# Row sums of the router weights by one matmul on chip instead of a pass through DRAM, and several steps moved in the order of a Strassen-like pipeline

## The chip, the cores and the metric

The kernel runs on one core of a Trainium2 chip. The metric is device time in microseconds (us), the median of several executions. TensorE is PE in the profile, VectorE is DVE, ScalarE is ACT, GpSimd is POOL, SyncE is SP.

## The reference

The input x is 4 x 1024 tokens of 1024 features. Each token is normalized (mean and variance over its features) to xn, and two branches follow:

```
g    = sigmoid(xn @ gate_w.T + gate_b)
u_g  = xn * g
s_t  = running recurrence over the sequence of b*u_g with decay tanh(a)
y    = c*s + (d + low_rank(mean over sequence of u_g)) * u_g
p    = softmax(xn @ wr.T)            (8 experts), top 2, weights normalized
h    = silu(silu(xn @ w1.T) @ w3.T) @ w2.T
out[index_k of a token] += weight_k * h[token]     (rows 0 to 7 only)
result = x + y * silu(out)
```

The scatter lands in rows 0 to 7 of the first batch alone, since an expert's number is used as a row. So everything but those 8 rows is a copy of x. What is needed in full is h for all 4096 tokens, the router's choice for all tokens, and the mean of u_g over the first batch.

## The kernel before

**The products.** Each 1024 x 1024 x 1024 product is done with seven half-size products (Strassen's scheme in Winograd's form) instead of eight. Every operand is split in a high part and a low part (`h`, `l`), both in fp32r, and each step is three matmuls: high by high, high by low, low by high (`three`, lines 926 to 928). There are nine stages, n = 0 to 8: stages 0 to 3 are x @ w1.T for the four batches, stage 4 is the gate for the first batch, stages 5 to 8 are the product with w3. A stage has seven products (n, i), each of four tiles j, each tile of 12 matmuls of 512 columns. `TILES` lists them by (n, p, j), where p is the position of the product in its stage. Every engine's program is one loop over this list, and `at` = (p, j) says at which tile an engine issues each other step; an engine takes its steps strictly in this order and waits at each for its semaphores. So a place in the list is an order on that engine's own queue, and no time.

**The steps around the products.** DVE forms the sums of blocks that the scheme needs (`x_sum(n, k)`, `w_sum`), ACT rounds them to the high part (`high`, `weights`), DVE subtracts to get the low part (`low(n, i)`, `low_weights`). Each works on a 128 x 2048 tile. DVE also adds finished PSUM tiles to running sums (`evict`). Product (n, i) waits once, ahead of its first matmul, for `low(n, i)` and `low_weights` (`x_in`, `w_in` in `product`). Within DVE's loop at stages 4 and 5 the order was:

```
(0,1): x_sum(n,1)            [stage 4: then two_greatest()]
(0,3): x_sum(n,2), x_sum(n,4)
(1,0): w_sum(n-3,4), low_weights(n-3,2)
(1,1): low(n,2), x_sum(n,3)
(1,2): low_weights(n-3,3)
```

**The router.** `logits(n, b)` multiplies raw x block b (a, c, b, d) by wr, 32 small matmuls each. They run after tile (1,3) in stage 0 and after tile (0,3) in stages 1 to 3. `logits_turned` transposes them to tokens by experts on DVE. The x of the two batches of stages 0 and 1 is raw, so their logits are corrected afterwards: `logits_normalized` subtracts mean times the row sum of wr and multiplies by the inverse deviation, 12 short linked DVE steps; `two_greatest` then picks the experts and `shares` their weights. The row sums of wr came from ACT: job "wr" in `JOBS` loads wr, line 740 sums its rows, SP writes the 8 sums to DRAM (`sums_out`, line 510) and reads them back to all partitions (`sums_back`, line 514). `row_sums` jobs also give the token statistics and the row sums of w1.

**The aggregation.** `aggregate(n, i, of)` multiplies activated tiles by the router's weights into two PSUM banks, 8 small matmuls per j. In stage 8 the ones of i = 1, 4, 5 run after tile (6,1), the one of i = 6 at the very end, before `last_product`.

Of the kernel before, what the change touches and what calls it, by code (L numbers as in the profile page):

```python
# [5 lines left out]
P = 128  # L6
D = 1024
KT = D // P
TOK = 4096
SEQ = 1024  # L10
UT = 1024
HT = 512
E = 8
# [7 lines left out]
GATE = 4  # L21
L2 = 5
# [7 lines left out]
FOLDED = tuple(n for n in SOURCE if SOURCE[n] < RAW)  # L30


JOBS = [(u, r) for u in (2, 3, 0, 1) for r in range(KT)] + [("wr", 0)]
JOBS += [("w1", r) for r in range(KT)]
PLACES = 9
BANKS = 5

# [115 lines left out]
PART = counts(*((b, k) for b in "ac" for k in range(PIECES[b])))  # L153


def program(nc, x, xT, xa, wB, w11, w1, wr, w2T, small, out):
    loads, loaded = {}, [0] * PLACES
    for n in range(NN):
        for b in "acbd" if n else "bd":
# [16 lines left out]

    xh_d = nc.dram_tensor("xh_d", (2, 2, P, 4, HT), F32).ap()
    H_d = nc.dram_tensor("H_d", (NU, 2, 2, P, 4, HT), F32).ap()
    sw_d = nc.dram_tensor("sw_d", (E, 1), F32).ap()
    mv_d = nc.dram_tensor("mv_d", (2 * NU, 2, HT), F32).ap()  # L180

    with ExitStack() as ctx:
        def sb(name, shape, dt=F32):
            return ctx.enter_context(nc.sbuf_tensor(name, shape, dt))
# [4 lines left out]
        def sem(name):  # L189
            return ctx.enter_context(nc.semaphore(name))  # L190
# [27 lines left out]
        nm = sb("nm", [P, 1])  # L218
        acs = sb("acs", [P, 2 * NU, 2, 4])
        ws = sb("ws", [P, KT])  # L220
        wrs = sb("wrs", [P, 1])
        sw = sb("sw", [P, E])
        hb = sb("hb", [P, KT])
        aa = sb("aa", [P, KT])
        us = sb("us", [P, 2, KT])
# [18 lines left out]
        def piece(buf, c0, m, n):  # L244
            return buf[:, c0:c0 + m * n].rearrange("p (m n) -> p m n", n=n)
# [22 lines left out]
        lgp = [ps(f"lgp{i}", [P, HT]) for i in range(2)]  # L268
        spare = ps("spare", [P, HT])
        acc = [lgp[1], spare]  # L270

        s_row = [sem(f"s_row{i}") for i in range(2)]
        s_pl = [sem(f"s_pl{i}") for i in range(PLACES)]
# [17 lines left out]
        s_wh = sem("s_wh")  # L291
        s_wo = sem("s_wo")
        s_s = sem("s_s")
        s_sws = sem("s_sws")
        s_swl = sem("s_swl")
        s_fd = sem("s_fd")
        s_fs = sem("s_fs")
        s_mm = sem("s_mm")
# [40 lines left out]
        def job_buf(q):  # L339
            return rows[:, q % 2, :]  # L340
# [4 lines left out]
        def job_done(on, q):  # L345
            on.wait_ge(s_st2, q + 1)
# [113 lines left out]
        def bank_free(on, n, i, j):  # L460
# [7 lines left out]
            else:  # L468
# [4 lines left out]
            [(0, *at) for at in ((2, 1), (2, 3), (3, 0), (3, 1), (3, 3), (4, 0), (4, 2), (5, 0), (6, 0), (6, 2))]  # L473
            + [(1, *at) for at in ((0, 1), (0, 3), (1, 2), (2, 2), (3, 2), (4, 1), (5, 1), (6, 0), (6, 2))]
            + [(2, *at) for at in ((0, 1), (0, 3), (1, 2), (2, 2), (3, 0), (3, 2), (4, 1), (5, 1), (6, 0), (6, 2))]
            + [(3, *at) for at in ((0, 1), (0, 3), (1, 1), (1, 3), (2, 2), (3, 0), (3, 2), (4, 1), (5, 0), (5, 2), (6, 0),
                                   (6, 2))])}
        turned_at = {(0, 4, 0): 4, (0, 6, 0): 5, (2, 1, 3): 6, (2, 5, 1): 7, (3, 1, 3): 0, (3, 2, 3): 1, (3, 3, 3): 2,
                     (3, 5, 1): 3}
        back_at = {(0, 4, 1): (2, 0), (0, 6, 1): (2, 1), (2, 2, 0): (3, 0), (2, 5, 2): (3, 1)}  # L480
# [11 lines left out]
        def _(eng):  # L492
            on = Waits(eng)

            def row(q):
                if q >= 2:
                    job_done(on, q - 2)
                of, r = JOBS[q]
                if of == "wr":
                    src = wr  # L500
                elif of == "w1":
                    src = w1[r * P:(r + 1) * P, :]
                else:
                    r0 = BATCH[of] * SEQ + r * P
                    src = x[r0:r0 + P, :]
                eng.dma_start(job_buf(q)[0:E, :] if of == "wr" else job_buf(q), src).then_inc(s_row[q % 2], 16)

            def sums_out():
                job_done(on, JOBS.index(("wr", 0)))
                eng.dma_start(sw_d, wrs[0:E, :]).then_inc(s_sws, 16)  # L510

            def sums_back():
                on.wait_ge(s_sws, 16)
                eng.dma_start(sw[:, :], sw_d.rearrange("e o -> (o e)").partition_broadcast(P)).then_inc(s_swl, 16)

            def first_block(b, k):
                src = xa[k] if b == "a" else part(xT[BATCH[0], 1, 0], b, k)
# [76 lines left out]
            for t in range(4, len(TILES)):  # L594
# [58 lines left out]
                    stats_out(turned_at[(n, p, j)])  # L653
                if (n, p, j) in back_at:
                    stats_back(*back_at[(n, p, j)])
                if n == GATE - 1 and at == (2, 0):
                    sums_out()
                if n == GATE - 1 and at == (3, 0):
                    sums_back()
                if (n, p, j) in save_at:  # L660
                    save(save_at[(n, p, j)])
                if n == NN - 1:
# [57 lines left out]
        def _(eng):  # L720
# [11 lines left out]
            def row_sums(q):  # L732
                job_loaded(on, q)
                of, r = JOBS[q]
                buf = job_buf(q)
                if of == "w1":
                    eng.activation(buf, buf, ACT.Copy, accum_out=ws[:, r:r + 1]).then_inc(s_st2, 1)
                    return
                if of == "wr":
                    eng.activation(buf[0:E, :], buf[0:E, :], ACT.Copy, accum_out=wrs[0:E, :]).then_inc(s_st2, 1)  # L740
                    return
                total, square = (acs[:, 2 * of + r // 4, e, r % 4:r % 4 + 1] for e in range(2))
                link(eng.activation(buf, buf, ACT.Copy, accum_out=total))  # L743
                link(eng.activation(nm[:, :], total, ACT.Copy, scale=-1.0 / D))
                eng.activation(buf, buf, ACT.Square, bias=nm[:, 0:1], accum_out=square).then_inc(s_st2, 1)  # L745
# [176 lines left out]
        def _(eng):  # L922
# [57 lines left out]
            def aggregate(n, i, of):  # L980
                o, h = OUT_OF[i]
                on.wait_ge(s_pz, 2)
                on.wait_ge(s_rt, 2 * NU)
                u = SOURCE[n]
                for j in of:
                    c_ready(on, n, i, j)
                    for q in range(NQ):
                        ins = eng.matmul(acc[o][Q * q:Q * (q + 1), 0:P].rearrange("p (k i) -> p k i", i=Q),  # L988
                                         Pz[:, 8 * u + 4 * h + j, :], in_group(c_buf(n, i, j), q),
                                         start=(n == L2 and h == 0 and j == 0), stop=(n == NN - 1 and h == 1 and j == 3))  # L990
                return ins
# [14 lines left out]
            for t in range(4, len(TILES)):  # L1006
                n, p, j = TILES[t]
                at = (p, j)
                product(*tile_of(t))
                if n == 0:  # L1010
                    if at == (1, 3):
                        for b in "acbd":
                            logits(0, b)
                if n in (1, 2, 3) and at == (0, 3):
                    for b in "acbd":
                        logits(n, b)
                if n == L2 and at == (3, 2):
                    on.wait_ge(s_um, 1)
                    on.wait_ge(s_one, 1)
                    on.wait_ge(s_rt, 2 * NU)  # L1020
                    eng.matmul(lgp[0][:, 0:RANK], ones, prs[:, :], start=True, stop=True).then_inc(s_at, 1)  # L1021
                if n > L2 and at == (0, 1):
                    for i in (1, 4, 5, 6):
                        aggregate(n - 1, i, range(4)).then_inc(s_ph, 1)
                if n == NN - 1 and at == (6, 1):
                    for i in (1, 4, 5):
                        aggregate(n, i, range(4)).then_inc(s_ph, 1)
            aggregate(NN - 1, 6, range(3))
            last_product(0, (4, 5))
            aggregate(NN - 1, 6, range(3, 4)).then_inc(s_ph, 1)  # L1030
# [4 lines left out]
        def _(eng):  # L1035
# [3 lines left out]
            def link(ins):  # L1039
                count[0] += 1  # L1040
                ins.then_inc(s_dv, 1)
                on.wait_ge(s_dv, count[0])
# [224 lines left out]
            def logits_turned(c):  # L1267
# [3 lines left out]
                link(eng.transpose(flat, lgp[c % 2][:, 0:P]))  # L1271
                eng.tensor_copy(L[:, 4 * c:4 * c + 4, :], flat.rearrange("p (j e) -> p j e", e=Q)[:, :, 0:E]).then_inc(s_rt, 1)

            def logits_normalized():

                on.wait_ge(s_rt, 2 * NU)
                on.wait_ge(s_swl, 16)
                on.wait_ge(s_mv, len(MV))
                for s in range(2 * RAW):
                    of = L[:, 4 * s:4 * s + 4, :]  # L1280
                    mean, rstd = (mvu[:, s, 4 * e:4 * e + 4].unsqueeze(2).to_broadcast([P, 4, E]) for e in range(2))
                    part_ = piece(lg[:, 0:P], 32 * s, 4, E)
                    link(tt(part_, mean, sw[:, :].unsqueeze(1).to_broadcast([P, 4, E]), ALU.mult))
                    link(tt(of, of, part_, ALU.subtract))
                    link(tt(of, of, rstd, ALU.mult))

# [78 lines left out]
            for t in range(4, len(TILES)):  # L1365
# [4 lines left out]
                if n == 0:  # L1370
                    if at == (1, 0):
                        low_weights(0, 3)
                    if at == (1, 1):
                        x_sum(0, 3)
                    if at == (1, 2):
                        low(0, 3)
                    if at == (1, 3):
# [38 lines left out]
                if n == L2 and at in ((0, 0), (0, 1)):  # L1416
                    gated(6, 2 + j)

                if n == GATE - 1 and at == (4, 1):
                    logits_normalized()  # L1420
                if n in (1, 2, 3):
                    if at == (1, 3):
                        logits_turned(2 * n)
                    if at == (3, 0):
                        logits_turned(2 * n + 1)

                if n in FOLDED and at == (0, 0):
# [7 lines left out]
                if at == (0, 3):  # L1435
                    x_sum(n, 2)
                    x_sum(n, 4)
                if at == (1, 1):
                    low(n, 2)
                    x_sum(n, 3)  # L1440
                if at == ((1, 3) if n < L2 else (2, 1)):
                    low(n, 3)
                if at == ((2, 1) if n < L2 else (2, 3)):
# [50 lines left out]

                if n == GATE:
                    if at == (0, 1):
                        two_greatest()
                    if at == (2, 1):
                        shares()
# [49 lines left out]
```

## Time and profile before

| what | value |
|---|---|
| median of 3 runs | 732.86 us (732.62 to 732.95) |
| the profiled execution's own time | 732.95 us |
| its span | 731.1 us |
| PE busy | 725.5 us, 99% |
| DVE busy | 516.7 us, 71% |
| ACT busy | 357.3 us, 49% |
| granted TensorE clock, mean | 1.00 |

The span runs from the first to the last instruction of the profile; 1.85 us of the execution's time lie outside it. Busy time of PE is that of its matmuls, overlapped ones counted once, so 99% says that PE hardly ever stood without one. It doesn't say that the other 29% of DVE are free where they would be needed.

### The profile page before, as it was taken

Reading aid. Unit: us, or ns where it says so; the run is one execution under the profiler, and the core shown is the slowest. Engines: PE = TensorE matmul, PEld = TensorE weight load, DVE = VectorE, ACT = ScalarE, POOL = GpSimd, SP = SyncE. Lnnn points to the kernel's source line nnn. Section 1 sums busy time; section 2 is a strip of 40 time slices with the busy share of each in tenths; the row PEclk is TensorE's granted clock in tenths of the full one; section 3 lists DMA queues with packets and bytes.
Section 4 is the critical chain, followed back from the end, with each engine's and each line's share of the span. In section 5 each row is a group of like instructions: output and inputs, shape, how many; then the busy total and the mean of one; then the engine's idle time right before and its main releaser. Section 6 shows DMA issues by size and latency. Waiting matters only on the chain.

```text
span 731.1 us, 9945 instructions
## 1 busy us (share of the span) xinstructions
PE 725.5 (99%) x4132; PEld 600.8 (82%) x4132; DVE 516.7 (71%) x500; ACT 357.3 (49%) x444; POOL 17.4 (2%) x37
## 2 busy tenths in 40 slices
PE   9999999999999999999999999999999999999997
PEld 7888888888888888888888888888888888888885
DVE  5798456748676686599989987654588756895421
ACT  6489648164745776355824653234244442462221
POOL 0001000000010010000000000000000000000000
PEclk9999999999999999999999999999999999999999
DMA  8636844678464847869676803260038103300240
GB/s 328 243 130 217 315 175 148 212 264 277 139 213 156 287 145 258 292 214 347 204 285 229 317 1 143 110 236 1 31 129 302 58 1 144 143 2 0 71 165 3
DMA packets 31117, 126.80 MB, mean 173 GB/s; under 512 B 4760, under 2 KB 4952, under 8 KB 23904
## 3 DMA queue, kind: packets, MB, share of 16 engines
q1 hardware_dynamic: 21824, 109.37, 42.3%
q10 hardware_dynamic: 9248, 16.80, 6.2%
q8 instruction: 32, 0.52, 0.3%
q14 instruction: 13, 0.11, 0.0%
HBM read 105.08 MB, written 37.78 MB: 195 GB/s over the span
## 4 chain that ended last, share of the span: by engine, by line
PE 99%; DMA 0%; DVE 0%; ACT 0%; issue 0%; DVEq 0%
PE main L926 32%; PE main L927 31%; PE main L928 31%; PE lgp L975 2%; PE lgp L988 1%; PE spare L988 1%; PE main L999 0%; DMA x0f<-xa 0%; DVE tail L1045 0%; DVE x3r L1045 0%; DVE wl0r L1045 0%; ACT x2r L749 0%; ACT u L916 0%; PE lgp L1021 0%; DVEq L90 0%
## 5 line engine op out<-in xcount | busy, mean ns | idle before, releaser
L1045 DVE TENSOR_TENSOR s<-s,main 128x512 f32<-128x512 f32 x72 | 48.5, 682 | 65.3 <-PE main L928 65.3
L1045 DVE TENSOR_TENSOR u<-u,main 128x512 f32<-128x512 f32 x36 | 24.1, 681 | 31.9 <-PE main L928 31.8
L784 ACT ACTIVATE s<-main 128x512 f32<-128x512 f32 x36 | 20.7, 593 | 46.6 <-PE main L928 24.8
L809 ACT ACTIVATE rows<-rows 128x512 f32<-128x512 f32 x16 | 10.0, 632 | 65.6 <-DVE rows L1045 65.6
L1045 DVE TENSOR_TENSOR u<-s,main 128x512 f32<-128x512 f32 x32 | 21.6, 683 | 25.7 <-PE main L928 25.7
L745 ACT ACTIVATE rows<-rows,nm 128x1024 f32<-128x1024 f32 x32 | 36.9, 1153 | 1.0
L743 ACT ACTIVATE rows<-rows 128x1024 f32<-128x1024 f32 x32 | 33.5, 1047 | 2.7 <-DMA rows<-x 2.6
L809 ACT ACTIVATE s<-s 128x512 f32<-128x512 f32 x24 | 15.0, 631 | 40.5 <-DVE s L1045 40.5
L809 ACT ACTIVATE u<-u 128x512 f32<-128x512 f32 x24 | 15.0, 628 | 34.2 <-DVE u L1045 34.2
L1045 DVE TENSOR_TENSOR rows<-s,main 128x512 f32<-128x512 f32 x16 | 10.8, 685 | 22.0 <-PE main L928 22.0
L927 PE MATMUL main<-x7r,wh2r 128*128 128x512 f32 x48 | 18.7, 389 | 0.0
L926 PE MATMUL main<-x2r,wh0r 128*128 128x512 f32 x32 | 12.9, 403 | 0.2 <-DVE wl0r L1045 0.2
L767 ACT ACTIVATE x3r<-x7f 128x2048 fp32r<-128x2048 f32 x2 | 3.8, 1922 | 18.2 <-DVE x6f L1045 15.6
L928 PE MATMUL main<-x2r,wl0r 128*128 128x512 f32 x32 | 12.7, 397 | 0.0
L928 PE MATMUL main<-wh3r,x6r 128*128 128x512 f32 x32 | 12.5, 390 | 0.0
L927 PE MATMUL main<-x5r,wh1r 128*128 128x512 f32 x32 | 12.5, 390 | 0.0
L927 PE MATMUL main<-wl5r,x4r 128*128 128x512 f32 x32 | 12.5, 389 | 0.0
L927 PE MATMUL main<-x6r,wh0r 128*128 128x512 f32 x32 | 12.5, 389 | 0.0
L927 PE MATMUL main<-wl2r,x4r 128*128 128x512 f32 x32 | 12.5, 389 | 0.0
L926 PE MATMUL main<-x6r,wh3r 128*128 128x512 f32 x32 | 12.5, 389 | 0.0
L927 PE MATMUL main<-x8r,wh3r 128*128 128x512 f32 x32 | 12.5, 389 | 0.0
L928 PE MATMUL main<-x6r,wl3r 128*128 128x512 f32 x32 | 12.5, 389 | 0.0
(645 smaller groups left out, 2371.4 us busy)
## 6 DMA issues: line engine op xcount, KB each, us to landing
rows<-x SPq DMA_DIRECT2D x32, 512.0 KB, 4.5
out<-x SPq DMA_DIRECT2D x31, 512.0 KB, 10.6
H_d<-u ACTq DMA_DIRECT2D x32, 256.0 KB, 5.0
bc<-mv_d SPq DMA_DIRECT2D x8, 512.0 KB, 4.4
H_d<-s ACTq DMA_DIRECT2D x16, 256.0 KB, 5.0
rows<-w SPq DMA_DIRECT2D x8, 512.0 KB, 4.2
rows<-xh_d SPq DMA_DIRECT2D x16, 256.0 KB, 5.2
w2f<-w2T SPq DMA_DIRECT2D x2, 2048.0 KB, 10.4
```

The costliest lines, as they stand in the source:

```text
L743: link(eng.activation(buf, buf, ACT.Copy, accum_out=total))
L745: eng.activation(buf, buf, ACT.Square, bias=nm[:, 0:1], accum_out=square).then_inc(s_st2, 1)
L767: eng.activation(xr(n, f"h{i}"), xf(n, x_from(n, i)), ACT.Copy).then_inc(s_hi, 1)
L784: eng.activation(s1[:, j, :], bk, ACT.Copy).then_inc(s_pa, 1)
L809: eng.activation(c, c, ACT.Silu).then_inc(s_sl, 1)
L926: eng.matmul(o, sh, mh, start=first, stop=False, skip_group_check=True)
L927: eng.matmul(o, sh, ml, start=False, stop=False, skip_group_check=True)
L928: return eng.matmul(o, sl_, mh, start=False, stop=last, skip_group_check=True)
L975: ins = eng.matmul(lgp[h][Q * q:Q * (q + 1), 0:P].rearrange("p (j i) -> p j i", i=Q), wr32[:, 4 * kh + k, :], in_group(xf(n, b)[:, k, :], ...
L988: ins = eng.matmul(acc[o][Q * q:Q * (q + 1), 0:P].rearrange("p (k i) -> p k i", i=Q), Pz[:, 8 * u + 4 * h + j, :], in_group(c_buf(n, i, j) ...
L1045: return eng.tensor_tensor(o, a, b, op)
```

## The change

The row sums of wr are made on the chip. DVE reduces the padded wr, which lies in SBUF with the other small inputs, to 128 x 8 partial sums at (1,1) of stage 0; PE multiplies them by a matrix of ones right behind stage 0's logits, into the bank `spare`; DVE reads them there. The "wr" job, both DMAs and their semaphores go, and the jobs of stage 3 move a little. Beside this five steps move: `logits_normalized` goes from (4,1) of stage 3 to (0,1) of stage 4, directly ahead of `two_greatest`; the logits of stage 1 are split and go from (0,3) to (0,1) (blocks a, c) and (1,1) (blocks b, d); their transposes go from (1,3) and (3,0) to (2,0) and (4,0); `x_sum(n, 3)` goes from (1,1) to (1,0) in stages 4 and 5; the aggregation of i = 1 and 4 in stage 8 goes from (6,1) to (5,1).

```diff
-JOBS = [(u, r) for u in (2, 3, 0, 1) for r in range(KT)] + [("wr", 0)]
-JOBS += [("w1", r) for r in range(KT)]
+JOBS = [(u, r) for u in (2, 3, 0, 1) for r in range(KT)] + [("w1", r) for r in range(KT)]
...
-        wrs = sb("wrs", [P, 1])
-        sw = sb("sw", [P, E])
+        wrs = sb("wrs", [P, E])
...
+        wr_sums = spare[:, 0:E]
...
-            + [(3, *at) for at in ((0, 1), (0, 3), (1, 1), (1, 3), (2, 2), (3, 0), (3, 2), (4, 1), (5, 0), (5, 2), (6, 0),
-                                   (6, 2))])}
+            + [(3, *at) for at in ((0, 1), (0, 3), (1, 2), (2, 2), (3, 0), (3, 2), (4, 1), (5, 0), (5, 2), (6, 0), (6, 2))])}
...
-                if n == GATE - 1 and at == (2, 0):
-                    sums_out()
-                if n == GATE - 1 and at == (3, 0):
-                    sums_back()
...
@@ tensor
                     if at == (1, 3):
                         for b in "acbd":
                             logits(0, b)
-                if n in (1, 2, 3) and at == (0, 3):
+                        on.wait_ge(s_one, 1)
+                        on.wait_ge(s_sw, 1)
+                        eng.matmul(wr_sums, ones, wrs[:, :], start=True, stop=True).then_inc(s_wm, 1)
+                if n == 1 and at == (0, 1):
+                    logits(1, "a")
+                    logits(1, "c")
+                if n == 1 and at == (1, 1):
+                    logits(1, "b")
+                    logits(1, "d")
+                if n in (2, 3) and at == (0, 3):
...
+                if n == NN - 1 and at == (5, 1):
+                    for i in (1, 4):
+                        aggregate(n, i, range(4)).then_inc(s_ph, 1)
                 if n == NN - 1 and at == (6, 1):
-                    for i in (1, 4, 5):
-                        aggregate(n, i, range(4)).then_inc(s_ph, 1)
+                    aggregate(n, 5, range(4)).then_inc(s_ph, 1)
@@ vector
+            def sums_of_wr():
+                on.wait_ge(s_cst, 16)
+                eng.tensor_reduce(wrs[:, :], wr32[:, :, 0:E].rearrange("p k e -> p e k"), AX.X, ALU.add).then_inc(s_sw, 1)
...
             def logits_normalized():
 
                 on.wait_ge(s_rt, 2 * NU)
-                on.wait_ge(s_swl, 16)
+                on.wait_ge(s_wm, 1)
                 on.wait_ge(s_mv, len(MV))
+                on.wait_ge(s_ln, LN[(GATE - 1, "d")])
...
-                    part_ = piece(lg[:, 0:P], 32 * s, 4, E)
-                    link(tt(part_, mean, sw[:, :].unsqueeze(1).to_broadcast([P, 4, E]), ALU.mult))
+                    part_ = rest[:, 4 * s:4 * s + 4, :]
+                    link(tt(part_, mean, wr_sums.unsqueeze(1).to_broadcast([P, 4, E]), ALU.mult))
...
                     if at == (1, 1):
                         x_sum(0, 3)
+                        sums_of_wr()
...
-                if n == GATE - 1 and at == (4, 1):
-                    logits_normalized()
                 if n in (1, 2, 3):
-                    if at == (1, 3):
+                    if at == ((2, 0) if n == 1 else (1, 3)):
                         logits_turned(2 * n)
-                    if at == (3, 0):
+                    if at == ((4, 0) if n == 1 else (3, 0)):
                         logits_turned(2 * n + 1)
...
+                if n in (GATE, L2) and at == (1, 0):
+                    x_sum(n, 3)
                 if at == (1, 1):
                     low(n, 2)
-                    x_sum(n, 3)
+                    if n not in (GATE, L2):
+                        x_sum(n, 3)
...
                     if at == (0, 1):
+                        logits_normalized()
                         two_greatest()
```

## Rows read from the trace of the kernel before

**Rows 1.** The page: busy time of TensorE, and the chain that ended last, by engine.

```profile
PE 725.5 (99%) x4132; PEld 600.8 (82%) x4132; DVE 516.7 (71%) x500; ACT 357.3 (49%) x444; POOL 17.4 (2%) x37
...
PE 99%; DMA 0%; DVE 0%; ACT 0%; issue 0%; DVEq 0%
```

**Rows 2.** Timeline of PE, stage 0: start us, us, engine, line, operation, out<-in, count.

```profile
26.16 0.39 PE L928 MATMUL main<-x4r,wl1r 128*128 128x512 f32 x1
...
28.20 0.39 PE L928 MATMUL main<-x4r,wl1r 128*128 128x512 f32 x1
...
29.41 1.06 PE L975 MATMUL lgp<-x1f,cst 128*32 128x128 f32 x32
...
31.16 1.06 PE L975 MATMUL lgp<-x7f,cst 128*32 128x128 f32 x32
...
33.41 0.39 PE L928 MATMUL main<-x2r,wl3r 128*128 128x512 f32 x1
```

**Rows 3.** Windows: us, busy of PE, PEld, DVE, ACT, POOL, then PEclk, DMA, GB/s.

```profile
297.90:300.60 2.70, 2.70 (x14) 2.23 (x13) 2.30 (x13) 1.67 (x3) 0.00 (x0) 1.00 1.01 425
337.90:348.78 10.88, 10.88 (x49) 9.01 (x48) 10.78 (x5) 7.88 (x8) 0.00 (x0) 1.00 0.78 287
```

**Rows 4.** Timeline of DVE in stages 0 and 1: two waits.

```profile
28.67 2.29 DVE L1045 TENSOR_TENSOR x3r<-x8f,x2r 128x2048 fp32r<-128x2048 f32 x1 [1.98 <-ACT x2r L767]
...
99.20 2.29 DVE L1045 TENSOR_TENSOR x2f<-x8f,x2f 128x2048 f32<-128x2048 f32 x1 [11.25 <-PE lgp L975]
```

**Rows 5.** Timeline of PE in stage 5, around the one-off product of line 1021.

```profile
443.76 0.40 PE L928 MATMUL main<-wh3r,x6r 128*128 128x512 f32 x1
443.99 0.28 PE L1021 MATMUL lgp<-prs,lg 128*128 128x4 f32 x2
...
446.74 0.39 PE L928 MATMUL main<-wh3r,x6r 128*128 128x512 f32 x1
```

**Rows 6.** Timeline of PE in stage 8, around its last full aggregation group.

```profile
713.98 0.39 PE L928 MATMUL main<-wh6r,x0r 128*128 128x512 f32 x1
...
718.32 0.39 PE L928 MATMUL main<-wh6r,x0r 128*128 128x512 f32 x1
```

**Rows 7.** Timeline of DVE, stages 3 and 4; in brackets the idle time before.

```profile
316.34 0.69 DVE L1045 TENSOR_TENSOR u<-u,main 128x512 f32<-128x512 f32 x1 [1.78 <-PE main L928]
...
337.80 2.29 DVE L1045 TENSOR_TENSOR x4f<-x4f,x3f 128x2048 f32<-128x2048 f32 x1
...
340.01 2.28 DVE L1045 TENSOR_TENSOR wl6f<-wl6f,wl2f 128x2048 f32<-128x2048 f32 x1
...
344.61 2.29 DVE L1045 TENSOR_TENSOR x3r<-x3f,x2r 128x2048 fp32r<-128x2048 f32 x1
346.81 2.29 DVE L1045 TENSOR_TENSOR x8f<-x0f,x8f 128x2048 f32<-128x2048 f32 x1
```

**Rows 8.** Timeline of DVE and PE at the start of the kernel.

```profile
4.99 0.69 DVE L1045 TENSOR_TENSOR wl0r<-wl2f,wh0r 128x512 fp32r<-128x512 f32 x1
...
5.83 0.77 PE L926 MATMUL main<-x2r,wh0r 128*128 128x512 f32 x1 [0.17 <-DVE wl0r L1045]
...
6.82 0.63 PE L928 MATMUL main<-x2r,wl0r 128*128 128x512 f32 x1
...
7.25 0.44 PE L926 MATMUL main<-x2r,wh0r 128*128 128x512 f32 x1
```

**Rows 9.** Timeline of PE: the first matmul of product (4,2).

```profile
348.78 0.39 PE L926 MATMUL main<-x2r,wh2r 128*128 128x512 f32 x1
```

**Rows 10.** Timeline of ACT in stage 4: the step that waits for two_greatest.

```profile
343.57 0.22 ACT L875 ACTIVATE bc<-bc 128x32 f32<-128x32 f32 x1
```

**Rows 11.** Timeline of DVE and of PE in stages 4 and 5.

```profile
376.18 0.69 DVE L1045 TENSOR_TENSOR x6f<-s,main 128x512 f32<-128x512 f32 x1 [2.03 <-PE main L928]
...
419.86 2.28 DVE L1045 TENSOR_TENSOR x0r<-x0f,x4r 128x2048 fp32r<-128x2048 f32 x1
...
424.94 0.39 PE L926 MATMUL main<-wh2r,x4r 128*128 128x512 f32 x1
```

More of the change, by code:

```diff
@@ L153, with program @@
 PART = counts(*((b, k) for b in "ac" for k in range(PIECES[b])))
-def program(nc, x, xT, xa, wB, w11, w1, wr, w2T, small, out):
+def program(nc, x, xT, xa, wB, w11, w1, w2T, small, out):
     loads, loaded = {}, [0] * PLACES
@@ L178, in program @@
     H_d = nc.dram_tensor("H_d", (NU, 2, 2, P, 4, HT), F32).ap()
-    sw_d = nc.dram_tensor("sw_d", (E, 1), F32).ap()
     mv_d = nc.dram_tensor("mv_d", (2 * NU, 2, HT), F32).ap()
@@ L293, in program @@
         s_s = sem("s_s")
-        s_sws = sem("s_sws")
-        s_swl = sem("s_swl")
+        s_sw = sem("s_sw")
+        s_wm = sem("s_wm")
         s_fd = sem("s_fd")
@@ L498, in row @@
                 of, r = JOBS[q]
[L499 to L514, printed above, removed]
+                r0 = r * P if of == "w1" else BATCH[of] * SEQ + r * P
+                eng.dma_start(job_buf(q), (w1 if of == "w1" else x)[r0:r0 + P, :]).then_inc(s_row[q % 2], 16)
             def first_block(b, k):
@@ L737, in row_sums @@
                     eng.activation(buf, buf, ACT.Copy, accum_out=ws[:, r:r + 1]).then_inc(s_st2, 1)
-                    return
-                if of == "wr":
-                    eng.activation(buf[0:E, :], buf[0:E, :], ACT.Copy, accum_out=wrs[0:E, :]).then_inc(s_st2, 1)
                     return
@@ L1539 @@
         "w1": np.ascontiguousarray(t["L0_ffn_w1"]),
-        "wr": np.ascontiguousarray(t["L0_ffn_wr"]),
         "w2T": np.ascontiguousarray(t["L0_ffn_w2"].T),
```

## The prediction

> **What bounds the kernel now.** First the page: TensorE is busy 99% of the span, and the chain that ended last is 99% TensorE with none of it on DVE, ACT or DMA [rows 1]. So only two things move the time: work or switches put on TensorE's own queue, and moments in which TensorE would have to stand. Nothing taken from ACT, the DMA queues or DVE can make it shorter by itself. Next the timeline of PE for its cadence: from 26.16 to 28.20 us nine steps pass, 0.227 us for one 512-column matmul [rows 2]. Last, since no wait on TensorE is left to find in the list of waits, DVE's timeline at each place that the change touches, read against the moment at which TensorE needs the result. DVE has 29% idle on average, but between 337.90 and 348.78 it is busy 10.78 of 10.88 us [rows 3], and it is there that steps are added.
>
> **The change part by part.**
>
> *Row sums of wr, what goes.* One short ACT job and two small DMAs in stage 3. None lies on the chain [rows 1]. Value: 0; below nothing it can't go either, for TensorE never waits there. The jobs of stage 3 that move are ACT's, with the same excuse.
>
> *Row sums of wr, what comes.* DVE's reduction over 64 values stands behind `x_sum(0, 3)` in stage 0, and DVE idles 1.98 us right behind that, from 26.69 to 28.67, until ACT has rounded x [rows 4]. A step of some 0.2 us is swallowed there; without this cover it would delay `low(0, 3)` by as much. It ends near 27 us, and PE, which now waits for it behind the logits, comes there at 31.16 + 0.88 = 32.04 [rows 2], so that wait is free. The matmul itself costs. The nearest row is the one-off product with the same 128 x 128 ones and 4 columns: from 443.76 to 446.74 twelve steps pass, 2.98 us against 12 x 0.227 = 2.72, so 0.26 us [rows 5]. That one paid for leaving the main stream, this one stands where the stream is already left; and 8 columns take the place of 4. I take 0.26, with 0.05 and 0.45 as ends.
>
> *Logits of stage 1 split.* The same 128 small matmuls, but in two groups. What does a group cost beside its matmuls? From the main matmul at 28.20 to the sixth behind the group at 33.41 are 5.21 us; six steps of 0.227 make 1.36, and two groups of 32 take 31.16 - 29.41 = 1.75, so four take 3.50; 0.35 is left for leaving and coming back [rows 2]. In stage 8 with three groups of 32: 718.32 - 713.98 = 4.34, less 1.36 and 2.63, again 0.35 [rows 6]. One more group: +0.35 (ends 0.25 and 0.45). On DVE, `x_sum(1, 1)` waited 11.25 us for block a's logits [rows 4] and now waits two tiles less (24 x 0.227 = 5.4). Then it waits at `x_sum(1, 3)` for block b's. They come, from a group that began about 98.1 us, two tiles, a group of 64 (2.1) and their own 0.9 later: 106.5. Before, DVE took that step four steps of some 2.3 us behind 99.20, at 108.4. Nothing in stage 1 gets later, and as TensorE didn't wait there nothing is won. The transposes of two groups move behind with them.
>
> *Aggregation of stage 8 split.* Blocks 1 and 4 at (5,1), their inputs long activated by then; again one group more, +0.35. The end of the kernel behind the last main matmul is as before.
>
> *`x_sum(n, 3)` earlier, stages 4 and 5.* It goes ahead of `w_sum`, `low_weights(n-3, 2)` and `low(n, 2)`. A step of this size takes 346.81 - 344.61 = 2.20 us of DVE from start to start [rows 7]. Product (n, 2) waits for `low(n, 2)`.
>
> *`logits_normalized` from stage 3 to stage 4.* Twelve linked steps fill 297.90 to 300.60, 2.70 us [rows 3]. Where it stood, DVE was ahead of TensorE: at 316.34 it still idles 1.78 us for a tile [rows 7], so taking it away makes nothing behind 316.34 earlier. Where it goes, DVE runs back to back from 316.34 to the end of `low(4, 2)`: this is the queue in which every microsecond counts. Its four reads of PSUM in place of SBUF may add up to 0.2 us; I leave them at 0.
>
> *Both together at product (4,2).* `low(4, 2)` starts at 344.61 and ends at 346.90 [rows 7]. From such an end to the matmul that waits for it, the one instance at the start shows 0.15 us (4.99 + 0.69 = 5.68 to 5.83 [rows 8]), so ready at 347.05. TensorE comes to the product at 348.78 [rows 9]: slack 1.73 us. Added ahead: 2.70 + 2.20 = 4.90 us. TensorE therefore stands 4.90 - 1.73 = 3.17 us, and the work behind it can't give that back. Both queues have the same shift up to 316.34, so the earlier terms don't alter it. Ends: 2.9 (a few gaps between linked steps lost) and 3.5 (PSUM reads, a later release). Queued behind the stalled product is all of TensorE. What hangs on DVE next is `low_weights(1, 3)` and `low(4, 3)`: `x_sum(4, 3)` is then behind us, so they are 2.70 late and TensorE 3.17, and their slack grows. ACT's step that waits for `two_greatest` at (1,0) of stage 4 began at 343.57 [rows 10], and DVE was past `two_greatest` before 337.80 [rows 7], so 2.70 later is still in time.
>
> *The same at product (5,2).* `low(5, 2)` ends at 419.86 + 2.28 = 422.14 and TensorE comes at 424.94 [rows 11]: slack 2.65 with the same 0.15. Added: 2.20. So 0.45 is left and there is no stall. DVE's lateness of stage 4 doesn't reach there: at 376.18 it idles 2.03 us for TensorE [rows 11].
>
> *A clock term.* In the rows of the start, TensorE's matmuls of 512 columns lie 7.25 - 6.82 = 0.43 us apart [rows 8], twice the later 0.227, which is the lower level of its clock (1.2 GHz) before it rises to 2.4 GHz. The row of 337.90 to 348.78 has a granted clock of 1.00 [rows 3]. Could a stand of 3.17 us bring it down? No row of before has such a stand. The Trainium skill, "TensorE: Matmul & The Clock Gate", section "The HAM clock gate", says that the lower level is the default and that an engine left idle long enough falls back to it until it has been busy again. By that rule the stall might cost more than its length; the time is worked out as a rival below, from rows. My sum has 0 for it.
>
> *Sum.* 0.35 + 0.35 + 0.26 + 3.17 = 4.13 us. On the profiled execution's 732.95: 737.08. That one lay 0.09 above the median of the runs shown, so 737.0.
>
> **The rivals.** A, the forecast: 737.0, own range 736.4 to 737.8 by the ends above (4.13 less 0.68, and plus 0.7).
>
> B, not slower by more than can be told: product (4,2) doesn't wait, since DVE reaches it early enough. The place is the same, the price of being right is 3.17, and it decides at 1.73 us of additions ahead of `low(4, 2)`. It would need DVE to begin its run 3.17 us sooner, for instance because the 5 us less of waiting in stage 1 and the 2.70 less in stage 3 are carried forward. For it speaks that DVE's total is unchanged and 71% [rows 1]; against it that DVE idles for TensorE's tile at 316.34 [rows 7], so nothing saved before is carried past that. Left would be 0.35 + 0.35 + 0.26 = 0.96: 733.8.
>
> C, the clock falls in the stall. At the start the lower spacing lasts from the first seen at 5.83 to 7.25 [rows 8], which is 1.42 us at half rate, a loss of 0.7; if it held from the span's start to 7.25, the loss of such a stretch is half of that, 3.6. So 737.7 to 740.6, middle 739.2. For it: the start. Against it: 0.17 us and all other breaks here leave the clock up, but they are much shorter.
>
> D, a second stall: the 0.45 us at (5,2) is too little, or an evict of stage 4 comes too late for its PSUM bank. Up to 2.20 more if the slack is misread as a whole, 0.3 to 1 likelier: 737.6, up to 739.2. For it: DVE is without idle time there. Against it: TensorE is late by more than DVE.
>
> **How the numbers follow.** A 0.70, B 0.10, C 0.10, D 0.08, and 0.02 for a gain I see no place for. Predicted 737.0, the time of A. The range 735.9 to 738.5 takes in A, D for the most part, the near third of C, and a stall of half the length; B and the far end of C are outside, under 2 in 10. This kernel can be told from no change to about 0.2%, 1.5 us: B lies within it. Slower 0.88, same 0.10, faster 0.02.
>
> **What would show it.** TensorE idle about 3.2 us ahead of the first matmul of (4,2), released by DVE's low part of x, near 352.5 us where it was 348.8. DVE without a gap from the eviction at 316 to there, with twelve short steps and `x_sum(4, 3)` ahead. One group of small matmuls more in stage 1 and in stage 8, 0.35 each. One matmul of 8 columns near 32 us that costs about 0.26. No idle at (5,2). The granted clock at 1.00 behind the stall; matmuls 0.43 apart there would be C. Wrong altogether if TensorE has no wait in stage 4.

## The result, and the profile after

The changed kernel takes 739.29 us in the median (738.48 to 740.18, 4 runs) against 732.90 for the kernel before: 1.0088 times as long, 95% interval 1.007 to 1.0105, or +6.4 us. That is slower, as forecast, but past the forecast 737.0 and outside the range 735.9 to 738.5. The profiled execution took 739.49 us, with a span of 737.7. By the mean granted clock of the whole execution the five lie in order: 738.48 us with 1.000, 739.27 and 739.31 with 0.998, the profiled 739.49 with 0.996, 740.18 with 0.994.

The page after: busy times, and the chain by engine (before: [rows 1]).

```profile
PE 727.9 (99%) x4134; PEld 601.0 (81%) x4134; DVE 517.1 (70%) x501; ACT 356.1 (48%) x442; POOL 19.8 (3%) x37
...
PE 92%; DVE 4%; DMA 1%; issue 1%; SPq 1%; ACT 0%; DVEq 0%
```

The page alone would mislead: PE still reads 99%, and its busy time grew by 2.4 us with two more matmuls. What matters is that the chain has now 4% DVE. The list of TensorE's waits says where.

```profile
PE main L902 <- DVE x3r L1032: 3.0, 1, 3.0
PE spare L909 <- POOL ident L670: 1.6, 1, 1.6
PE main L902 <- issue: 0.3, 1, 0.3
PE main L902 <- ACT s L760: 0.2, 1, 0.2
```

The first row is new, and by far the longest of those that are; the last two lie in the first 60 us. DVE's timeline shows how it came about (before: [rows 7]); what is to be seen is that there is no idle time in brackets behind 316.83, that the twelve short steps fill 330.84 to 333.53, and that `x8f<-x0f,x8f`, which is `x_sum(4, 3)`, now stands ahead of `x3r`, the low part of product (4,2).

```profile
316.83 0.69 DVE L1032 TENSOR_TENSOR u<-u,main 128x512 f32<-128x512 f32 x1 [1.78 <-PE main L904]
...
330.84 0.18 DVE L1032 TENSOR_TENSOR bc<-mvu,spare 128x32 f32<-128x32 f32 x1
...
333.53 0.42 DVE L1288 TENSOR_REDUCE bc<-L 128x32 f32<-128x256 f32 x1
...
343.21 2.28 DVE L1032 TENSOR_TENSOR x8f<-x0f,x8f 128x2048 f32<-128x2048 f32 x1
...
350.01 2.29 DVE L1032 TENSOR_TENSOR x3r<-x3f,x2r 128x2048 fp32r<-128x2048 f32 x1
```

TensorE's timeline around it (before: [rows 9]):

```profile
349.05 0.39 PE L904 MATMUL main<-x5r,wl1r 128*128 128x512 f32 x1
352.44 0.47 PE L902 MATMUL main<-x2r,wh2r 128*128 128x512 f32 x1 [3.00 <-DVE x3r L1032]
...
353.43 0.43 PE L903 MATMUL main<-x3r,wh2r 128*128 128x512 f32 x1
353.67 0.63 PE L904 MATMUL main<-x2r,wl2r 128*128 128x512 f32 x1
354.09 0.63 PE L902 MATMUL main<-x2r,wh2r 128*128 128x512 f32 x1
...
356.65 0.58 PE L902 MATMUL main<-x2r,wh2r 128*128 128x512 f32 x1
357.07 0.40 PE L903 MATMUL main<-x3r,wh2r 128*128 128x512 f32 x1
357.31 0.40 PE L904 MATMUL main<-x2r,wl2r 128*128 128x512 f32 x1
```

From 349.05 to 352.44 are 3.39 us where one step of 0.227 should be: 3.16 us of stall. The matmuls up to 353.67 start at nearly the usual spacing (five steps in 1.23 us); then, from 353.67 to 357.07, eight steps are 0.43 us apart in place of 0.227, and 1.6 us more are gone (3.40 - 8 x 0.227). The windows of this stretch (us; busy PE, PEld, DVE, ACT, POOL; PEclk, DMA, GB/s) show a granted clock of 0.53 there, almost wholly the lower level, 1.2 GHz:

```profile
348.78:353.40 4.62, 1.62 (x7) 1.05 (x7) 4.62 (x5) 4.62 (x5) 0.00 (x0) 1.00 0.00 0
353.40:357.00 3.60, 3.60 (x10) 2.83 (x9) 3.60 (x4) 3.60 (x3) 0.00 (x0) 0.53 0.32 89
357.00:360.00 3.00, 3.00 (x14) 2.44 (x13) 2.96 (x8) 1.30 (x1) 0.00 (x0) 0.99 0.36 96
```

The third loss is at the very end. The last DMA issues of the kernel after, and the DMA queues from there to the end of the span (packets, MB, share):

```profile
734.42 0.66 SPq L660 DMA_DIRECT2D out<-tail  x2
734.43 1.26 ACTq L895 DMA_DIRECT2D out<-tail  x2
```

```profile
q10 hardware_dynamic: 32, 0.02, 2.3%
q1 hardware_dynamic: 32, 0.02, 2.3%
q14 instruction: 1, 0.01, 0.9%
```

The same of the kernel before:

```profile
728.70 0.66 SPq L681 DMA_DIRECT2D out<-tail  x2
728.70 0.98 ACTq L919 DMA_DIRECT2D out<-tail  x2
```

```profile
q10 hardware_dynamic: 32, 0.02, 3.2%
q1 hardware_dynamic: 32, 0.02, 3.1%
```

After, ACT needs 1.26 us for its two issues where it needed 0.98, an instruction load of 8 KB falls into the last 3.3 us, and from the issue to the end of the span are 3.28 us (737.7 - 734.42) in place of 2.40 (731.1 - 728.70). Spans are given to 0.1 us, so this difference of 0.88 is good to 0.1. Over all fourteen traces the stretch is 3.2 to 3.3 us in the six that have the load there and 2.4 to 2.5 us in the eight that don't, so I take 0.8. The load isn't a new one, it is one that came earlier before: from 640 to 700 us the instruction queue has two packets before and one after.

```profile
q14 instruction: 2, 0.02, 0.1%
```

```profile
q14 instruction: 1, 0.01, 0.1%
```

After, the packet moves between 736.0 and 736.6, behind ACT's second issue, which ended at 734.43 + 1.26 = 735.69. So it doesn't lie between the two issues, as the expectation of experiment 5 has it.

### The profile page after: what moved, and what is told of

Same layout as the page of the kernel before. It is cut to its first block, busy times and chain, and to the rows that moved or that the text cites. A ratio compares the mean times of both kernels' runs of the same rounds, so it can differ in the third digit from the quotient of the medians.

```text
span 737.7 us, 9945 instructions
## 1 busy us (share of the span) xinstructions
PE 727.9 (99%) x4134; PEld 601.0 (81%) x4134; DVE 517.1 (70%) x501; ACT 356.1 (48%) x442; POOL 19.8 (3%) x37
## 4 chain that ended last, share of the span: by engine, by line
PE 92%; DVE 4%; DMA 1%; issue 1%; SPq 1%; ACT 0%; DVEq 0%
PE main L902 29%; PE main L904 29%; PE main L903 29%; PE lgp L951 2%; DMA wl6f<-wB 1%; PE lgp L964 1%; PE spare L964 1%; PE main L975 0%; DVE bc L1032 0%; SPq L501 0%; DVE x3f L1032 0%; DVE x3r L1032 0%; DVE x1r L1032 0%; DVE x8f L1032 0%; DVE wl6f L1032 0%
## 5 line engine op out<-in xcount | busy, mean ns | idle before, releaser
L902 PE MATMUL main<-wh5r,x4r 128*128 128x512 f32 x32 | 12.6, 393 | 0.0
```

The source lines that it names most:

```text
L902: eng.matmul(o, sh, mh, start=first, stop=False, skip_group_check=True)
```

## The experiments

Twelve kernels. "Before" is the kernel before, run beside each: 732.88, 732.61 and 732.68 us in the three sets, in this order.

**1. The normalization back in stage 3** (of the changed kernel)

```diff
+                if n == GATE - 1 and at == (4, 1):
+                    logits_normalized()
...
                     if at == (0, 1):
-                        logits_normalized()
                         two_greatest()
```

> The changed kernel with the normalization of the logits back in stage 3. Theory (the stall at product (4,2) is additions minus slack, and a stall of 3.2 us also lowers TensorE's clock): 2.20 - 1.73 = 0.5 us of stall, no matmuls 0.43 us apart behind it, and about 735.0 us. Rival (the low clock and the extra time come with any stall there, or sit elsewhere): 0.5 us of stall and still some 1.5 us of slow matmuls, about 736.5 us.

The edit also gives the steps back their old scratch tile and drops the wait that came with the new one. Measured: 734.97 us (734.20 to 735.60). In its trace the step at (4,2) is 0.69 us long, so 0.46 of stall, and no matmuls lie 0.43 us apart. The stall theory holds, and with so short a stall the slow matmuls don't come; the mean clock is 0.999 or 1.000 in all eight executions.

**2. `x_sum(4, 3)` back behind `low(4, 2)`**

```diff
-                if n in (GATE, L2) and at == (1, 0):
+                if n == L2 and at == (1, 0):
...
-                    if n not in (GATE, L2):
+                    if n != L2:
```

> The changed kernel with x_sum(4, 3) back at (1,1) of stage 4. Theory: 2.70 - 1.73 = 1.0 us of stall, no low clock, about 735.5 us. Rival (the gathering of short linked steps is what hurts, not the sum of DVE time): nearly the whole 3.2 us stay, about 737 to 739 us.

Measured: 736.20 us (735.99 to 736.29). At (4,2) the step is 1.17 us, so 0.94 of stall as expected; but the time is 0.7 above the expectation. TensorE's timeline shows a second stall that I hadn't seen, ahead of tile 1 of product (4,4):

```profile
374.47 0.39 PE L904 MATMUL main<-x5r,wl4r 128*128 128x512 f32 x1
375.29 0.50 PE L902 MATMUL main<-x5r,wh4r 128*128 128x512 f32 x1 [0.43 <-DVE u L1032]
```

0.82 - 0.23 = 0.6 us, released by DVE's eviction of tile (4,3,1), whose PSUM bank the next product starts anew. This is rival D's mechanism. In the changed kernel it doesn't show, since there TensorE is later by more.

**3. Both back**

> The changed kernel with both steps of stage 4 back in their old places; groups and row sums of wr stay as changed. Theory: no stall at (4,2), granted clock 1.00, about 734.0 us: two groups of 0.35 and 0.1 to 0.25 for the product of wr's sums. Rival (the 0.9 us that came at the very end of the changed kernel's trace belongs to the change): about 734.9 us.

Measured: 734.05 us (733.84 to 734.92), +1.2, and no stall in stage 4. From 739.29 that is 5.2 us less: the two moves on DVE made four fifths of the loss. The end of its trace still takes 3.2 us, so the late instruction load isn't the moves'. That the median met the 734.0 of the theory is in part luck, for the theory left that end out: by the parts, two groups 0.7, the product 0.2 and the end 0.8, +1.7 was due. The trace shows what made up for it: TensorE begins product (0,4) at 53.81 us where it was 54.22 before, 0.4 earlier, and over all fourteen traces this moment lies anywhere from 53.36 to 54.84. So what lies ahead of it spreads the traces by up to 1.5 us, of which the product of wr's sums can be 0.2.

**4. Both back, and both groups undivided**

> As the one before, and both groups of small matmuls on TensorE undivided again (logits of stage 1, aggregation of stage 8), so that only the row sums of wr and the x_sum move of stage 5 are left of the change. Theory: 0.7 us below the one before, 733.1 us, the same as the kernel before within 0.3 us. Rival (a split group costs nothing, since the stream waits elsewhere anyway): no difference to the one before.

Measured: 733.91 us (733.46 to 734.72), +1.0; 0.14 below the one before where 0.7 were expected. The traces disagree with that: from TensorE's first matmul of product (0,4) to its last main matmul are 722.69 - 53.81 = 668.88 us in experiment 3 and 722.99 - 54.84 = 668.15 here, 0.73 less. Ahead of (0,4) TensorE meets DVE and waits by an amount that goes with how the first loads came in, and here it waited 0.4 and there not at all. So the medians of this pair leave the price of a group open; experiment 7 takes it up. And since this kernel stands 1.0 above before with next to nothing left of the change, it points to the end.

**5. ACT's program lengthened** (experiment 4 with four tiny steps at ACT's start)

```diff
-            eng.activation(nm[:, :], mhalf[:, 0:1], ACT.Silu)
+            for _ in range(5):
+                link(eng.activation(nm[:, :], mhalf[:, 0:1], ACT.Silu))
```

> The kernel with stage 4 and the groups back (only the row sums of wr and the x_sum move of stage 5 left of the change), with four tiny ACT steps more at the start, where ACT waits for data anyway, so that ACT's program is about as long as before. Every trace of the changed program so far has an 8 KB instruction load between the issues of the last output rows, and 3.2 to 3.3 us from the first issue to the end in place of 2.40. Theory (the load falls there because ACT's program got shorter): the load moves away, 2.4 us again, and about 733.0 us. Rival (it is SP's program, or the load is no cause): still 3.2 us and 733.9 us.

Measured: 732.98 us (732.58 to 734.23), ratio 1.0006 [0.9998, 1.0015]. The instruction load is gone from the end and ACT's issues take 0.97 us, with 2.46 to the end:

```profile
728.38 0.66 SPq L660 DMA_DIRECT2D out<-tail  x2
728.39 0.97 ACTq L896 DMA_DIRECT2D out<-tail  x2
```

**6. SP's program lengthened** instead (eight more waits on a semaphore long reached)

```diff
+            for _ in range(8):
+                eng.wait_ge(s_x0["a"][0], 16)
             for t in range(4, len(TILES)):
```

> The same kernel with eight more waits in SP's program, on a semaphore long reached, and no change of ACT's. Theory (ACT's program): the load and the 3.2 us stay, 733.9 us. Rival (SP's program): 2.4 us and 733.0 us.

Measured: 733.86 us (733.24 to 734.69), ratio 1.0014 [1.0005, 1.0022], ACT's issues 1.27 us, the load is there. Together with 5, from the same set, this shows the cause: with more instructions for ACT the kernel is 0.9 us faster than with more for SP, and though the two intervals overlap, the traces show where the time is: 2.4 us at the end against 3.2. By taking the "wr" job off ACT the change moved a load of ACT's instructions from stage 8 into the last output. The Trainium skill, "Runtime: NRT & Kernel Launch", section "Instruction fetch mechanics", says that each engine's sequencer fetches its instructions by DMA page by page and that the cost of a boundary is mostly hidden. The trace agrees with the fetching (the instruction queue's packets above); that it was hidden doesn't hold here, where nothing stands behind it: 0.8 us.

**7. The split groups alone** (on the kernel before)

> The kernel before with the two split groups alone: logits of stage 1 in two groups, aggregation of stage 8 in two. The traces show 0.35 us more per group, but undoing both moved the median by only 0.14 us in the run with groups back. Theory (0.35 each is real, and that comparison was blurred by where stage 0 waits): +0.7 us, 0.1%. Rival (a split group costs less than its trace says): +0.2 us or less.

Measured: 733.84 us (733.12 to 735.17), ratio 1.0015 [1.0006, 1.0024], so +0.4 to +1.8 us with 1.2 in the middle. The groups are not free, and that answers the rival; 0.7 lies within. The trace, from product (0,4) to the last main matmul, has 722.74 - 53.81 = 668.93 us against 722.40 - 54.22 = 668.18 before: 0.75 for both. The rest of the 1.2 is within the spread of the start.

**8. Two extra reductions on DVE ahead of `low(4, 2)`** (on the kernel before)

```diff
                     if at == (1, 0):
+                        for _ in range(2 if n == GATE else 0):
+                            link(eng.tensor_reduce(prs[:, :], xf(n, "f"), AX.X, ALU.add))
                         w_sum(n - 3, 4)
```

> The kernel before with two extra DVE reductions over 2048 elements (about 2.25 us each) at (1,0) of stage 4, ahead of w_sum; nothing else changed. Theory: 4.5 - 1.73 = 2.8 us of stall at (4,2), 0.6 us or a little more at (4,4) for an evicted bank as in the run with x_sum back, and in some executions up to 1.7 us of matmuls at half rate: 736.3 to 738 us. Rival (the low clock belongs to something else in the change): granted clock 1.00 and 736.3 us in all executions.

Measured: 737.01 us. The stall is 3.12 - 0.23 = 2.89 us, and at (4,4) again 0.6. Its five executions: 736.21 and 736.39 with a mean granted clock of 1.000, and 737.01, 737.39, 737.68 with 0.998, 0.997, 0.996. So this stall brings the clock down in two of five, and most likely in a third: a mean of 0.998 alone is no proof, since experiment 3, which has no stall, shows it too (at 733.90 and 734.74 us), but 0.6 us more than the slower of the first two speaks for it.

**9. Three extra reductions**

> The same with three such reductions. Theory: 6.75 - 1.73 = 5.0 us of stall, 0.6 at (4,4), and the low clock in every execution, 1.7 us lost: about 740.2 us. Rival (no clock term): 738.5 us.

Measured: 739.38 us (738.76 to 739.99), clock 0.998 or less in all four executions. The windows of its trace:

```profile
347.60:353.00 5.40, 0.41 (x2) 0.00 (x0) 5.30 (x4) 0.00 (x0) 0.00 (x0) 0.97 0.00 0
353.00:356.30 3.30, 3.23 (x8) 2.63 (x9) 3.30 (x4) 1.14 (x1) 0.00 (x0) 0.53 0.02 5
356.30:360.00 3.70, 3.70 (x18) 3.04 (x17) 3.70 (x4) 3.70 (x5) 0.00 (x0) 1.00 0.34 91
```

The stall is 5.22 us. Seven slow steps follow, 3.08 us where 1.59 were due:

```profile
353.07 0.77 PE L926 MATMUL main<-x2r,wh2r 128*128 128x512 f32 x1 [5.06 <-DVE x3r L1045]
...
356.15 0.40 PE L927 MATMUL main<-x3r,wh2r 128*128 128x512 f32 x1
```

So the slow time cost 1.5 us; the clock had begun to fall within the stall (0.97 in the first window), and that part of it cost nothing. There is no second stall at (4,4). The 0.8 under my expectation are for the most part this missing 0.6. That all four executions had a fall doesn't rest on their mean clocks alone: the trace of the fastest shows it, and the others took longer still.

**10. The two DVE moves alone** (on the kernel before)

> The kernel before with the DVE moves alone (normalization to (0,1) of stage 4, x_sum(n, 3) to (1,0) in stages 4 and 5). Theory: 3.2 us of stall at (4,2) and the half-rate matmuls in most executions: +3.2 without and +4.8 with them, median near 737.2 us; ACT's program has its old length, so 2.4 us at the end. Rival (the stall needs the other parts too): under +3.

Measured: 738.55 us (735.39 to 739.04), ratio 1.0071 [1.0058, 1.0085]. ACT's issues at the end take 0.98 us, with 2.46 to the end. The stall is 3.41 - 0.23 = 3.18 us. Here the low clock held for longer:

```profile
348.00:352.20 4.20, 1.18 (x4) 0.69 (x4) 4.20 (x5) 4.20 (x5) 0.00 (x0) 0.81 0.00 0
352.20:357.40 5.20, 5.20 (x14) 3.99 (x13) 5.20 (x5) 5.04 (x3) 0.00 (x0) 0.50 0.38 101
357.40:360.00 2.60, 2.60 (x13) 2.14 (x12) 2.57 (x7) 0.00 (x0) 0.00 (x0) 0.99 0.44 72
```

From 351.68 to 357.63, fourteen steps, are 5.95 us where 3.18 were due: 2.8 us. With the stall that makes 6.0, and the profiled execution lies 738.70 - 732.68 = 6.0 above before. The six executions lie apart as the clock does: 735.39 with 0.999, 737.35 with 0.997, and 738.44, 738.65, 738.70, 739.04 with 0.995. The first is +2.7 over before, close to the bare stall; the others add 2.0 to 3.7. The parts roughly make the whole: the moves 5.9, the groups about 0.7, the end 0.8 come to 7.4 against 6.4; the clock's spread is larger than this difference, so the sum is no finer test.

**11. The whole change, with ACT lengthened**

> The whole changed kernel with the four tiny ACT steps at the start. Theory: the instruction load at the end goes, 0.9 us less than the changed kernel: 738.4 us. Rival: 739.3 us as before.

Measured: 738.02 us (736.64 to 738.58), 0.98 us for ACT's issues; 1.3 below the changed kernel where 0.9 were expected, or about 1 with each taken against the kernel before of its own set (+5.3 and +6.4). In its trace the clock had fallen within the stall of 3.16 us, and the slow steps cost 1.5 us. Two of five executions are at 736.64 and 736.68 with a clock of 1.000, three at 738.02 to 738.58 with 0.997 or 0.998. In the changed kernel it was one of five, so the median may also hold less of the low clock, by chance.

**12. One group at the end** (on the kernel before)

```diff
-                if n == NN - 1 and at == (6, 1):
-                    for i in (1, 4, 5):
-                        aggregate(n, i, range(4)).then_inc(s_ph, 1)
-            aggregate(NN - 1, 6, range(3))
+            for i in (1, 4, 5):
+                aggregate(NN - 1, i, range(4)).then_inc(s_ph, 1)
+            aggregate(NN - 1, 6, range(4)).then_inc(s_ph, 1)
             last_product(0, (4, 5))
-            aggregate(NN - 1, 6, range(3, 4)).then_inc(s_ph, 1)
```

> The kernel before with the aggregation of i = 1, 4, 5 in stage 8 moved to the end, so that all four stand in one group behind the last main matmul, where TensorE waits for DVE and ACT anyway. By the theory of the group's price (0.35) and the 0.27 us of idle there: 0.5 to 0.6 us less than before, 732.2 us. Rival (the small matmuls at the end lengthen the chain that ends last by more than that): no change or slower.

The edit also moves one of DVE's transposes, `aggregate_turned(1)`, behind the last eviction. Measured: 732.24 us (731.92 to 733.66) against 732.68; ratio 0.9997 [0.9988, 1.0005]. The trace has what was meant, one group without a hole:

```profile
718.70 0.39 PE L928 MATMUL main<-wh6r,x0r 128*128 128x512 f32 x1
719.02 1.08 PE L988 MATMUL lgp<-x3f,bc 128*32 128x128 f32 x32
...
721.67 1.06 PE L988 MATMUL lgp<-s,bc 128*32 128x128 f32 x32
722.54 3.64 PE L999 MATMUL main<-w2f,tail 128*32 128x256 f32 x64
```

The median is 0.44 lower and the span 1.0 shorter, but the interval includes no change: likely a little better than before, not shown. Of the 1.0 us 0.6 lie ahead of product (0,4) (53.63 against 54.22); from there to the first output issue are 727.63 - 53.63 = 674.00 us against 728.70 - 54.22 = 674.48, so the grouping itself gained 0.5 in the trace.

## Why the prediction was wrong

| term | forecast, us | found | by |
|---|---|---|---|
| stall at (4,2) | 3.17 | 3.16 | trace after; 0.46, 0.94, 3.18 in experiments 1, 2, 10 |
| low clock behind it | 0 | 1.6; 1.5, 2.8 and 1.5 in experiments 9, 10, 11; none in the trace of 8 | traces |
| one group more, twice | 0.70 | 0.73 and 0.75 in traces | 3 and 4, 7 |
| product of wr's sums | 0.26 | 0.24 where it stands, 0 behind the wait at (0,4) | trace after |
| DVE's part ahead of (0,4) | none | 0.13 | trace after |
| end of the kernel | 0 | 0.8 | 5 and 6 |
| stall at (5,2) | none | none | trace after |
| sum | 4.13 | 6.4 | |

- **Steps that held.** The stall came at the place and with the length forecast, from additions of 4.90 less a slack of 1.73. DVE's last idle time was again at the tile of 316, so neither the shorter wait in stage 1 nor the step taken from stage 3 was carried forward: rival B is out. At (5,2) the low part ended at 427.42 + 2.28 = 429.70 and TensorE took it at 430.31; less the 0.15 for the release 0.46 is left, as reckoned (before: [rows 11]). PSUM as a source for the normalization cost nothing, 0.22 us from step to step as before.
- **The step that failed: "My sum has 0 for it", of the clock.** I had the mechanism as rival C with a chance of 0.10, because no break in the trace of before had brought the clock down; but none of them was near 3 us, so they said nothing about it (and the one of 0.17 us that I named lies at 5.83, where the clock was still low). The runs put in its place: after a stall of 2.9 to 3.2 us the clock falls in most executions (by the mean clock four of five of the changed kernel, three of five in experiment 8, three of five in 11, five of six in 10, with the doubt on 0.998 told at 8), after 5.2 in all four, and after stalls of 0.5 and 0.9 no stretch of slow matmuls shows in the trace. C's price was 0.7 to 3.6; found are 1.5 to 2.8 in the four traces that have a fall. The Trainium skill, "TensorE: Matmul & The Clock Gate", section "The HAM clock gate", says that an engine left idle long enough falls back to the lower level, and the trace agrees: a granted clock of 0.53 behind the stall. In the trace after the clock fell only 1.2 us after TensorE had begun again, so there the end of the stall didn't save it.
- **The second: "The end of the kernel behind the last main matmul is as before."** I looked at which steps stand there and not at how an engine comes by its instructions. "Value: 0" for taking the job off ACT was wrong with it: this removal cost 0.8 us, by way of the place at which a load falls.
- **The wr product** was sized right, but I missed that TensorE waits for DVE at (0,4) in the trace of before, 0.41 - 0.23 = 0.18 us long. In the trace after TensorE came there at 53.70 and went on at 54.35, 0.13 behind the 54.22 of before. In both it goes on 0.1 us after DVE's low part of the weights (51.83 + 2.29 = 54.12 before, 51.95 + 2.29 = 54.24 after), so in this trace the wait swallowed the product whole, and the 0.13 is DVE's. DVE had it before its new reduction: its step at 17.92 us, which waits for a DMA, starts at 18.05 after. In experiments 2, 3, 5 and 11 no such wait shows, and there the 0.24 count.
- **Rival D** didn't occur in the changed kernel, but is real: 0.6 us at (4,4) in experiments 2 and 8.
- **The range.** With C given its true weight the likeliest time had been A plus 1.5, and the upper end 740. I had drawn it at 738.5 by calling C's far half unlikely. That the measured 739.29 is almost C's middle of 739.2 is luck: C's share of it is 1.6, and the end's 0.8, of which C knows nothing, makes up the rest.

## What to carry to other kernels

On a kernel whose chain is one engine, find the runs in which a helper engine has no idle time ahead of a step that the main engine waits for; what is added there less the slack gave the stall to 0.01 us in the changed kernel and to 0.03 in experiments 1 and 2, and the helper's average load said nothing. Then price what a stall does beside its length: in this kernel's stream holes of 2.9 to 5.2 us on TensorE brought half-rate matmuls behind them in most executions, 1.5 to 2.8 us of them in the traces, so spread the times by that. A step removed from an engine with nothing to do can still cost, when the loads of its instructions come at other moments; compare the last issues and the instruction queue of both traces.

## What the hardware showed unexpectedly

The same program, the same stall, and a clock that falls or doesn't: six executions of experiment 10 are spread over 3.7 us, in step with their mean clock, where the kernel before spreads over 1.7 in 23 runs. The lower clock can set in before the stall ends (experiment 9: seven slow steps behind 5.22 us of stall) or 1.2 us behind its end (the trace after), and what it costs depends on that and on how long it holds (seven or eight slow steps in three traces, fourteen in experiment 10). And one load of 8 KB of instructions among the last output issues costs 0.8 us.
